# Moving three of twelve tiles from VectorE to ScalarE in a threshold search

## The chip, the cores and the metric

One core of one Trainium2 chip runs the kernel. The metric is the device time of one execution in microseconds (us), and lower is better. Three executions of the kernel before stand beside each other, with their median. A fourth was recorded by the profiler.

## What is computed

A block of a vision transformer: 64 images are cut into patches and embedded (37 tokens of 192 numbers each, 2368 tokens in all), attention is added, and then a mixture of 8 experts with two experts for each token. The part that the change touches decides which tokens an expert keeps:

```python
w = softmax(topv)                     # weights of the two chosen experts
priority = w[:, 0]
order = jnp.argsort(-priority)
...
pos = (jnp.cumsum(oh, axis=0) * oh).sum(-1) - 1
keep = pos < cap                      # cap = 740 tokens for each expert
```

An expert keeps its 740 tokens of highest priority. The kernel does not sort. For each expert it looks for the priority of the last token that is kept, as a number of six digits to the base 16, one digit at a level.

## The kernel before

The tokens lie in 22 tiles of 111 (`NG` tiles, `G` = 111; three images to a tile). Embedding and attention fill the first 360 us of the profile, the experts' two matrix products the time from about 418 us on. Between them lies the routing, a chain of short steps that hand over from engine to engine.

**The tables of the search.** For each of the 8 experts `mp` holds the priority of every token that chose it. `mpb` repeats each of these 16 times, so that 8 x 16 = 128 columns stand for (expert, trial digit). TensorE transposes `mpb` tile by tile (L935): a tile becomes 128 partitions by 111 tokens, and a semaphore, `s_mpt`, counts the tiles. Four tiles share a PSUM bank, in the order `TILE_BANKS`: tiles 0 to 3, 4 to 7 and 8 to 11 are in three neighbouring banks, tiles 12 to 21 in three others. VectorE owns the first twelve (`BY_DVE` = 12), ScalarE the last ten (`BY_ACT` = 10). ScalarE copies its ten out of PSUM into `mp_act` once, with three instructions (L1205), the last of which waits for tiles 20 and 21. Those two belong to the last attention step and come late (`EARLY` = 20).

**A level of the search** (`search`, six times, `LEVELS` = 6). In each partition there is a threshold `thr`. VectorE counts how many of its 1332 values exceed it (L1659, read straight from PSUM, the sum in `cnt`) and turns the count into a bar (L1662, `cnt_bar`). Beside it, ScalarE takes the sign of threshold minus value for its 1110 values and sums the signs (L1213, `sgn_sum`). VectorE waits for this sum and compares it with the bar (L1665, `enough`). TensorE adds the outcomes of a group up to the digit (L950, into PSUM), and VectorE makes the next threshold from it (L1657), which starts both engines on the next level. At the first level the threshold is ready long before, and ScalarE does one more thing behind its sum, the copy `ohe` (L1217). Between two digits TensorE runs five matmuls that nobody reads (`keep_warm`, L792).

**Behind the search** come the last threshold (L1672, L954), the comparison with it (L1677, L1678), the running counts on TensorE (L959, L963), the table of slots on VectorE and TensorE (L1681 to L1718, with L972), and then the gathers of the first expert's rows on GpSimd (L1936), which wait for the table `gid`. The order on each engine is that of the code. `junk_v` and `junk_a` take the elementwise results, which nobody reads. They, `mp_act` and a few other tables are cut one behind the other from one piece of SBUF that the trace calls `narrow`; other pieces are cut from one called `wide`.

Of the kernel before, what the change touches and what calls it, by code (L numbers as in the profile page):

```python
# [8 lines left out]
BF16 = mybir.dt.bfloat16  # L9
# [3 lines left out]
ALU = mybir.AluOpType  # L13
ACT = mybir.ActivationFunctionType
# [15 lines left out]
G = IPG * T  # L30
# [30 lines left out]
WAYS, LEVELS = 16, 6  # L61
LEAST = -0.25 - 2.0 ** -24
HALF_ULP = 2.0 ** -25
BY_DVE = 12
BY_ACT = NG - BY_DVE
EARLY = NG - 2
REPEATS_DVE = ((0, 6), (6, 12))
REPEATS_ACT = ((12, 16), (16, 20))
TILE_BANKS = (4, 5, 6, 2, 7, 0)
# [34 lines left out]
def build(nc, x, ln1_g, ln1_b, W_lin, b_lin, ln2_g, ln2_b, pos_embedding, cls_token,  # L104
# [7 lines left out]
    with ExitStack() as ctx:  # L112
# [5 lines left out]
        def early(name, shape, dt=F32):  # L118

            return phase.enter_context(nc.sbuf_tensor(name, shape, dt))  # L120

        def sem(name):
            return ctx.enter_context(nc.semaphore(name))

        PS = ctx.enter_context(nc.psum_tensor("PS", [128, 8, 512], F32))
# [45 lines left out]
        def carve(memory):  # L171

            at = [0]

            def piece(parts, n, dt=F32):
                words = n if dt is F32 else n // 2
                a, at[0] = at[0], at[0] + words
                assert at[0] <= memory.shape[1]
                v = memory[0:parts, a:a + words]
                return v if dt is F32 else v.bitcast(dt)  # L180
            return piece
# [3 lines left out]
        piece = carve(wide)  # L185
        wraw = piece(128, 3 * NQKV).rearrange("p (b n) -> p b n", b=3)
        piece = carve(wide)
# [10 lines left out]
        piece = carve(wide)  # L198
# [4 lines left out]
        piece = carve(wide)  # L203
# [60 lines left out]
        thr = early("thr", [128, LEVELS])  # L264
# [16 lines left out]
        piece = carve(narrow)  # L281
# [9 lines left out]
        piece = carve(narrow)  # L291
        onehot = piece(G, 2 * NG * 128, FP16).rearrange("p (n j) -> p n j", n=128)
        row_no = piece(G, 2 * NG * 128, FP16).rearrange("p (n j) -> p n j", n=128)
        ohe = piece(G, 2 * NG * E, FP16).rearrange("p (e k g) -> p e k g", e=E, k=2)
        junk_v = piece(128, BY_DVE * G, BF16)
        junk_a = piece(128, BY_ACT * G, BF16)
        mp_act = piece(128, BY_ACT * G)
        tid = piece(128, E * NT)
        tvoid = piece(128, E * NT)
# [106 lines left out]
        s_mpr = sem("member_prios_repeated")  # L406
        s_tail = sem("row_tails_ready")
        s_mpt = sem("member_prios_psum")
        s_sgn = sem("signs_summed")
        s_enough = sem("enough_ready")  # L410
        s_dig = sem("digit_psum")
# [33 lines left out]
        def bc(ap, shape):  # L445
            return ap.to_broadcast(shape)
# [633 lines left out]
        def _(act):  # L1080
# [5 lines left out]
            for u in range(UNITS):  # L1086
# [5 lines left out]
                if u in (UNITS - 2, UNITS - 1):  # L1092
                    n = u - (UNITS - 2)
# [22 lines left out]
            def outputs(s, g):  # L1116
                act.wait_ge(s_otp[g], s + 1)
                nc.scalar.copy(oTh[:, g, :].rearrange("p (a n) -> p a n", a=2),  # L1118
                               PS[:, (6, 4)[g]:(8, 6)[g], 0:3 * G]).then_inc(s_oth[g], 1)
# [6 lines left out]
            def probs(s, g):  # L1126
                act.wait_ge(s_sh[g], s + 1)

                nc.scalar.activation(
                    pb[:, g, :].rearrange("p (h i t) -> p h i t", h=H, i=IPG),  # L1130
                    bc(sc[:, g, :].rearrange("p (h a t) -> p h a t", h=H, a=1), [G, H, IPG, T]),
                    ACT.Exp).then_inc(s_p[g], 1)

            def gate_rows(s):
                act.wait_ge(s_xrp, s + 1)
                nc.scalar.copy(xnT[:, :, :].rearrange("p k n -> p (k n)"), PS[0:KD, 3, 0:2 * G2]).then_inc(s_xrT, 1)

            def logits(s):
                act.wait_ge(s_lp, s + 1)
                nc.scalar.copy(logit[:, bass.ds(2 * s, 2), :],  # L1140
                               PS[0:G, 3, 0:2 * E].rearrange("p (g e) -> p g e", g=2)).then_inc(s_l, 1)

            def gap_exp(b_, at):
                act.wait_ge(s_d, b_ + 1)
                nc.scalar.activation(ex[:, at], ex[:, at], ACT.Exp).then_inc(s_e, 1)

            def last_step():

                s = STEPS - 1
                logits(s - 1)  # L1150
                probs(s, 0)
                act.wait_ge(s_sh[1], s + 1)
                nc.scalar.activation(pb[0:T, 1, :].rearrange("p (h i t) -> p h i t", h=H, i=IPG)[:, :, 0, :],
                                     sc[0:T, 1, :].rearrange("p (h t) -> p h t", h=H), ACT.Exp).then_inc(s_p[1], 1)
                outputs(s, 0)
                act.wait_ge(s_otp[1], s + 1)
                nc.scalar.copy(oTh[:, 1, :].rearrange("p (a c n) -> p a c n", a=2, c=3)[:, :, :, 0:T],
                               PS[:, 4:6, 0:3 * G].rearrange("p a (c n) -> p a c n", c=3)[:, :, :, 0:T]
                               ).then_inc(s_oth[1], 1)
                gap_exp(0, slice(0, EARLY))  # L1160
                gate_rows(s)
                logits(s)
                act.wait_ge(s_mp, 1)
                for a, z in REPEATS_ACT:
                    nc.scalar.copy(mpb[:, a:z], bc(mp[:, a:z, :].rearrange("p g (e a) -> p g e a", a=1),
                                                   [G, z - a, E, WAYS])).then_inc(s_mpr, 1)
                gap_exp(1, slice(EARLY, NG))
# [6 lines left out]
            def step(s):  # L1174

                before_ = not is_step(s, 0)
                if before_:
                    probs(s - 1, 0)
                if before_ and not is_step(s, 1):
                    logits(s - 2)  # L1180
                queries(s, qr, rrb, s_qr)
                queries(s, qw, rwb, s_q)
                if before_:
                    probs(s - 1, 1)
                relative(s, 0)
                relative(s, 1)
                for g in range(2):
                    if before_:
                        outputs(s - 1, g)
                    values(s, g)  # L1190
                rows_transposed(s + 1)
                if before_:
                    gate_rows(s - 1)
# [5 lines left out]
            with act.Fori(2, STEPS) as s:  # L1199
                step(s)  # L1200
            last_step()
            for n, bank in ((4, TILE_BANKS[3]), (4, TILE_BANKS[4]), (2, TILE_BANKS[5])):
                t = 4 * TILE_BANKS.index(bank)
                act.wait_ge(s_mpt, t + n)
                last = nc.scalar.copy(mp_act[:, (t - BY_DVE) * G:(t - BY_DVE + n) * G], PS[:, bank, 0:n * G])  # L1205
            last.then_inc(s_mpr, 1)
            act.wait_ge(s_mpr, 3)
            for n in range(LEVELS):
                if n == 0:
                    act.wait_ge(s_ktab, 1)  # L1210
                else:
                    act.wait_ge(s_thr, n)
                nc.scalar.activation(junk_a[:, :], mp_act[:, :], ACT.Sign, bias=thr[:, n:n + 1], scale=-1.0,  # L1213
                                     accum_out=sgn_sum[:, n:n + 1]).then_inc(s_sgn, 1)
                if n == 0:
                    act.wait_ge(s_mp, 4)
                    nc.scalar.copy(ohe[:, :, :, :], oh[:, :, :, :].rearrange("p k g e -> p e k g")).then_inc(s_ohe, 1)  # L1217
# [82 lines left out]
        def _(dve):  # L1300
            v = nc.vector

            def ch(ins):

                dve.drain()
# [345 lines left out]
            def search(n):  # L1651

                if n == 0:
                    dve.wait_ge(s_mpt, BY_DVE)
                else:
                    dve.wait_ge(s_dig, n)
                    v.tensor_tensor(thr[:, n:n + 1], PS[:, 3, 0:1], try_at[:, n:n + 1], ALU.add).then_inc(s_thr, 1)  # L1657
                    dve.wait_ge(s_thr, n)
                ch(v.tensor_scalar(junk_v[:, :].rearrange("p (a n) -> p a n", a=BY_DVE // 4),  # L1659
                                   PS[:, TILE_BANKS[0]:TILE_BANKS[0] + BY_DVE // 4, 0:4 * G], thr[:, n:n + 1], None, ALU.is_gt, ALU.add,  # L1660
                                   accum_out=cnt[:, n:n + 1]))
                ch(v.tensor_scalar(cnt_bar[:, n:n + 1], cnt[:, n:n + 1], 2.0, float(BY_ACT * G - 2 * CAP),  # L1662
                                   ALU.mult, ALU.add))
                dve.wait_ge(s_sgn, n + 1)
                v.tensor_tensor(enough[:, n:n + 1], sgn_sum[:, n:n + 1], cnt_bar[:, n:n + 1], ALU.is_le  # L1665
                                ).then_inc(s_enough, 1)

            dve.wait_ge(s_ktab, 1)
            for n in range(LEVELS):
                search(n)  # L1670
# [367 lines left out]
```

## Time and profile before

| | us |
|---|---|
| three executions | 611.55, 611.6, 614.45 |
| their median | 611.6 |
| the profiled execution, whole | 611.77 |
| its span, first to last instruction | 610.0 |
| the search, first sum on ScalarE to last digit | 373.2 to 387.7 |
| TensorE busy over the span | 539.3 (88%) |
| VectorE busy | 441.9 (72%) |
| ScalarE busy | 261.1 (43%) |

The shares are averages over stages that have different limits. TensorE is busy for 88% of the span, but in the stretch of the search it runs mostly the idle matmuls. What a change to the search is worth has to be read from its own 14.5 us.

### The profile page before, as it was taken

To read this page: it belongs to the slowest core of one execution; us is meant where nothing else is said; L and a number is where in the kernel's file an instruction comes from. 1 tells how busy PE (TensorE), PEld (TensorE's weight loads), DVE (VectorE), ACT (ScalarE), POOL (GpSimd) and SP (SyncE) were. 2 spreads that over 40 slices of the span, in tenths; PEclk is the share of its full clock that TensorE was granted. 3 is DMA by queue.
4 is the path that set the end of the run, shared out by engine and by line. 5 is a ranking of instruction groups with operands and counts; after the bars stand their busy time and mean duration, and the time that the engine had idled before them with its cause. 6 is when DMAs were issued, how large, how long until landed. Compare 5 with 4: busy or idle time off the path is not lost.

```text
span 610.0 us, 12448 instructions
## 1 busy us (share of the span) xinstructions
PE 539.3 (88%) x4254; PEld 502.6 (82%) x4258; DVE 441.9 (72%) x1028; ACT 261.1 (43%) x428; POOL 220.8 (36%) x209
## 2 busy tenths in 40 slices
PE   2999687999999999999999786658999999999982
PEld 2999587999989989999899673446899999999982
DVE  7889956577687776776877757564877777877753
ACT  1222443244342543443435105404685595585560
POOL 0266510202102012021020115017688787777463
PEclk9999797899999999999999767869999999999997
DMA  8798535111201202102012018403466466357160
GB/s 204 171 219 255 139 72 135 24 36 17 51 19 32 51 3 48 36 15 51 23 29 51 2 33 214 129 5 107 125 159 160 103 139 151 94 128 153 19 170 31
DMA packets 62009, 54.97 MB, mean 90 GB/s; under 512 B 29204, under 2 KB 52564, under 8 KB 61182
## 3 DMA queue, kind: packets, MB, share of 16 engines
q1 hardware_dynamic: 52830, 46.04, 29.6%
q0 software_dynamic: 9152, 8.59, 8.2%
q8 instruction: 14, 0.23, 0.2%
q14 instruction: 13, 0.11, 0.1%
HBM read 39.32 MB, written 18.27 MB: 94 GB/s over the span
## 4 chain that ended last, share of the span: by engine, by line
PE 47%; DVE 14%; ACT 13%; issue 9%; SPq 5%; DMA 4%; POOL 3%; DVEq 2%; POOLq 1%; ACTq 0%
PE PS L1058 7%; PE PS L757 7%; PE PS L734 6%; PE PS L713 5%; ACT wide L1105 4%; PE PS L1056 4%; ACT hTh L1246 3%; PE PS L741 2%; PE PS L750 2%; PE PS L748 2%; PE PS L749 2%; DVE hTl L1753 2%; PE PS L721 2%; PE PS L728 2%; PE PS L1033 2%
## 5 line engine op out<-in xcount | busy, mean ns | idle before, releaser
L1828 POOL TENSOR_TENSOR rs<-ve,nhalf 111x1 f32<-111x1 f32 (+2 forms) x40 | 26.1, 653 | 272.4 <-DVE ve L1396 189.5
L1962 POOL DMA_INDIRECT running_sums<-ye,gid x42 | 74.5, 1774 | 30.8 <-DVE ye L1777 21.7
L1058 PE MATMUL PS<-w2hl,hTh 128*128 128x384 f32 (+1 forms) x288 | 82.7, 357 | 0.0
L1056 PE MATMUL PS<-w2hl,hTl 128*128 128x192 f32 (+1 forms) x288 | 73.4, 255 | 3.7 <-DVE hTl L1753 3.7
L1936 POOL DMA_INDIRECT xe<-routed_rows,gid x48 | 53.2, 1109 | 43.5 <-DVE gid L1718 28.9
L1056 PEld LDWEIGHTS PS<-w2hl,hTl 128*128 128x128 f32 (+1 forms) x288 | 53.7, 187 | 6.0 <-issue 5.2
L1033 PE MATMUL PS<-xeT,w1h 128*128 128x370 f32 x252 | 56.0, 330 | 0.0
L1058 PEld LDWEIGHTS PS<-w2hl,hTh 128*128 128x128 f32 (+1 forms) x288 | 53.0, 184 | 0.5
L713 PE MATMUL PS<-xT,wh 128*128 128x222 f32 x264 | 47.5, 290 | 6.5 <-DVE xT L1410 6.5
L1753 DVE TENSOR_TENSOR hTl<-hf,hTh 128x740 fp32r<-128x740 f32 x42 | 39.0, 928 | 19.4 <-ACT hTh L1246 18.3
L713 PEld LDWEIGHTS PS<-xT,wh 128*128 128x128 f32 x264 | 38.5, 201 | 8.7 <-issue 5.9
L1033 PEld LDWEIGHTS PS<-xeT,w1h 128*128 128x128 f32 x252 | 44.2, 188 | 0.0
L682 PE MATMUL PS<-narrow 128*128 128x192 f32 x216 | 41.0, 343 | 3.0 <-ACT narrow L1090 3.0
L1033 PE MATMUL PS<-xeT,w1l 128*128 128x370 f32 x168 | 42.0, 331 | 0.0
L734 PE MATMUL PS<-wide 111*111 111x96 f32 x336 | 39.8, 283 | 1.2 <-DVE wide L1549 1.2
L682 PEld LDWEIGHTS PS<-narrow 128*128 128x128 f32 x216 | 37.6, 203 | 3.3 <-ACT narrow L1090 3.3
L734 PEld LDWEIGHTS PS<-wide 111*111 111x111 f32 x336 | 37.9, 196 | 2.1 <-DVE wide L1549 1.3
L1243 ACT ACTIVATE hf<-PS,b1s 128x740 f32<-128x740 f32 x42 | 36.7, 875 | 6.1 <-PE PS L1033 4.0
L1428 DVE SCALAR_TENSOR_TENSOR wide<-PS,ind,wide 111x296 f32<-111x296 f32 x64 | 33.6, 525 | 4.2 <-issue 0.2
L713 PE MATMUL PS<-xT,wl 128*128 128x222 f32 x176 | 35.1, 282 | 0.0
L1118 ACT CAST oTh<-PS 128x666 fp32r<-128x666 f32 x21 | 15.1, 718 | 45.6 <-PE PS L741 45.6
L748 PE MATMUL PS<-woh,oTh 128*111 128x192 f32 x126 | 33.5, 266 | 0.9 <-DVE oTl L1458 0.9
(257 smaller groups left out, 1319.0 us busy)
## 6 DMA issues: line engine op xcount, KB each, us to landing
wide<-x SPq DMA_DIRECT2D x24, 288.0 KB, 9.2
w1r<-L_ffn_W SPq DMA_DIRECT2D x16, 384.0 KB
rel_scores<-wide SPq DMA_DIRECT2D x66, 73.0 KB
w2r<-L_ffn_W SPq DMA_DIRECT2D x8, 576.0 KB, 4.4
w1r<-L_ffn_W SPq DMA_DIRECT2D x16, 192.0 KB
wide<-rel_scores SPq DMA_DIRECT2D x22, 111.0 KB, 2.2
out<-running_sums SPq DMA_DIRECT2D x1, 1776.0 KB, 7.7
h_tokens<-narrow SPq DMA_DIRECT2D x24, 72.0 KB, 2.8
```

The source lines that it names most:

```text
L682: last = pe.matmul(PS[:, 4 + u % 4, 0:D], xTt[:, u % 2, c, :], W_cen[:, c, :], start=(c == 0), stop=(c == PC - 1))
L713: last = pe.matmul(PS[:, bank, (m % 2) * G2:(m % 2 + 1) * G2], lhsT, xT[:, b_, :], start=(nth == 0 and m % 2 == 0), stop=(nth == len(BLOCK ...
L734: last = pe.matmul(heads(4 - 2 * g, V)[:, j, :], pT[:, g, j * G:(j + 1) * G], v_sb[:, g, h * V:(h + 1) * V], start=(j % HB == 0), stop=Tru ...
L748: pe.matmul(PS[0:G, g, 0:D], oTh[:, g, at], woh[:, c, :], start=(c == 0), stop=False)
L757: last = pe.matmul(PS[0:G, 2 * g + n, 0:HB * V], xT[:, b_, g * G:(g + 1) * G], (wh, wl)[w][:, b_, at:at + HB * V], start=(nth == 0), stop= ...
L1033: last = pe.matmul(PS[:, hidden_bank(c) + n, 0:HALF], (w1h, w1l)[hl][:, b_, w], xeT[:, b_, n * HALF:(n + 1) * HALF], start=(nth == 0), sto ...
L1056: pe.matmul(PS[0:n, bank, 0:D], hTl[:, c, at], w2hl[:, c, 0, :], start=(c == 0), stop=False, skip_group_check=True)
L1058: last = pe.matmul(PS[0:n, bank, 0:2 * D], hTh[:, c, at], both(w2hl[:, c, :, :]), start=False, stop=(c == HC - 1), skip_group_check=True)
L1243: last = nc.scalar.activation(hf[:, c % 2, :].rearrange("p (a n) -> p a n", a=2), src, ACT.Gelu, bias=b1s[:, p, c:c + 1])
L1753: v.tensor_tensor(hTl[:, c, :], hf[:, c % 2, :], hTh[:, c, :].bitcast(F32), ALU.subtract).then_inc(s_hl, 1)
L1936: p_.indirect_dma_start(xe[0:r, p, n, :], None, xr_dram, bass.IndirectOffsetOnAxis(ap=gid[0:r, e, n:n + 1], axis=0), bounds_check=B * T - ...
L1962: p_.indirect_dma_start(sums, at, ye[0:r, e % 2, n, :], None, bounds_check=B * T + NT * 128 - 1, oob_is_err=True, compute_op=ALU.add).then ...
```

## The change

`BY_DVE` goes from 12 to 9 and so `BY_ACT` from 10 to 13. VectorE now counts the first three tiles of each of its three banks, 9 x 111 = 999 values. The fourth tile of each bank (tiles 3, 7 and 11) goes to ScalarE, which copies the three with one instruction ahead of its other copies. VectorE's first count waits for that copy (`s_fourth`) in place of the twelfth transpose. ScalarE's sum covers 1443 values. The two junk tiles get one spare element, since their lengths are odd now. The constant in `cnt_bar` follows from `BY_ACT`.

```diff
-BY_DVE = 12
+BY_DVE = 9
 BY_ACT = NG - BY_DVE
...
+        s_fourth = sem("fourth_tiles_copied")
...
             last_step()
+            act.wait_ge(s_mpt, 12)
+            nc.scalar.copy(mp_act[:, 0:3 * G].rearrange("p (a n) -> p a n", a=3),
+                           PS[:, TILE_BANKS[0]:TILE_BANKS[0] + 3, 3 * G:4 * G]).then_inc(s_fourth, 1)
             for n, bank in ((4, TILE_BANKS[3]), (4, TILE_BANKS[4]), (2, TILE_BANKS[5])):
...
-                nc.scalar.activation(junk_a[:, :], mp_act[:, :], ACT.Sign, bias=thr[:, n:n + 1], scale=-1.0,
+                nc.scalar.activation(junk_a[:, 0:BY_ACT * G], mp_act[:, :], ACT.Sign, bias=thr[:, n:n + 1], scale=-1.0,
                                      accum_out=sgn_sum[:, n:n + 1]).then_inc(s_sgn, 1)
...
                 if n == 0:
-                    dve.wait_ge(s_mpt, BY_DVE)
+                    dve.wait_ge(s_fourth, 1)
...
-                ch(v.tensor_scalar(junk_v[:, :].rearrange("p (a n) -> p a n", a=BY_DVE // 4),
-                                   PS[:, TILE_BANKS[0]:TILE_BANKS[0] + BY_DVE // 4, 0:4 * G], thr[:, n:n + 1], None, ALU.is_gt, ALU.add,
+                ch(v.tensor_scalar(junk_v[:, 0:BY_DVE * G].rearrange("p (a n) -> p a n", a=3),
+                                   PS[:, TILE_BANKS[0]:TILE_BANKS[0] + 3, 0:3 * G], thr[:, n:n + 1], None, ALU.is_gt, ALU.add,
                                    accum_out=cnt[:, n:n + 1]))
```

On ScalarE, from the exponent of the last two tiles to the first cast of the experts' weights, the kernel before has these instructions in a row (`narrow` written from `PS` is `mp_act`, `narrow` written from `narrow` the junk, `sgn_sum` the sums):

```order
L1145 ACTIVATE ex<-ex 111x2
L1205 COPY narrow<-PS 128x444 x2
L1205 COPY narrow<-PS 128x222
L1213 ACTIVATE narrow,sgn_sum<-narrow,thr 128x1110
L1217 CAST narrow<-oh 111x352
L1213 ACTIVATE narrow,sgn_sum<-narrow,thr 128x1110 x5
L1223 CAST w1h<-w1r 128x2304
```

At the same place the changed kernel has these, with line numbers moved by the added lines:

```order
L1146 ACTIVATE ex<-ex 111x2
L1204 COPY narrow<-PS 128x333
L1209 COPY narrow<-PS 128x444 x2
L1209 COPY narrow<-PS 128x222
L1217 ACTIVATE narrow,sgn_sum<-narrow,thr 128x1443
L1221 CAST narrow<-oh 111x352
L1217 ACTIVATE narrow,sgn_sum<-narrow,thr 128x1443 x5
L1227 CAST w1h<-w1r 128x2304
```

One copy of 333 values stands ahead of the three others, and the six sums are longer by 333 values; nothing else changes its place. VectorE and TensorE keep every instruction where it was.

## Rows read from the trace of the kernel before

**Rows 1.** The page: its span, and the chain that ended last, by engine.

```profile
span 610.0 us, 12448 instructions
PE 47%; DVE 14%; ACT 13%; issue 9%; SPq 5%; DMA 4%; POOL 3%; DVEq 2%; POOLq 1%; ACTq 0%
```

**Rows 2.** The chain in order of time, through the search: start us, us, what.

```profile
372.35 0.42 PE PS L935 x2
372.80 0.35 ACT narrow L1205
373.17 1.32 ACT narrow L1213 x2
374.52 0.17 DVE enough L1665
...
374.95 0.17 DVE thr L1657
375.15 1.60 DVE narrow L1659
...
377.06 0.17 DVE enough L1665
...
377.51 0.17 DVE thr L1657
...
385.15 0.17 DVE thr L1657
```

**Rows 3.** VectorE's timeline: start us, us, instruction, shapes [idle before, releaser].

```profile
372.21 1.60 DVE L1659 TENSOR_SCALAR_CACHE_REDUCE narrow<-PS,thr 128x1332 bf16<-128x1332 f32 x1
...
374.52 0.16 DVE L1665 TENSOR_TENSOR enough<-sgn_sum,cnt_bar 128x1 bf16<-128x1 f32 x1 [0.47 <-ACT narrow L1213]
```

**Rows 4.** ScalarE's timeline, around the first level and at the sixth.

```profile
369.65 0.52 ACT L1205 COPY narrow<-PS 128x444 f32<-128x444 f32 x1
370.38 0.53 ACT L1205 COPY narrow<-PS 128x444 f32<-128x444 f32 x1 [0.21 <-PE PS L935]
372.80 0.34 ACT L1205 COPY narrow<-PS 128x222 f32<-128x222 f32 x1 [1.89 <-PE PS L935]
373.17 1.22 ACT L1213 ACTIVATE narrow<-narrow,thr 128x1110 bf16<-128x1110 f32 x1
374.30 0.19 ACT L1213 ACTIVATION_READ_ACCUMULATOR narrow<-narrow,thr 128x1 f32 x1
374.39 0.81 ACT L1217 CAST narrow<-oh 111x352 f16<-111x352 f32 x1
375.15 1.22 ACT L1213 ACTIVATE narrow<-narrow,thr 128x1110 bf16<-128x1110 f32 x1
...
385.35 1.22 ACT L1213 ACTIVATE narrow<-narrow,thr 128x1110 bf16<-128x1110 f32 x1 [1.24 <-DVE thr L1657]
386.47 0.19 ACT L1213 ACTIVATION_READ_ACCUMULATOR narrow<-narrow,thr 128x1 f32 x1
```

**Rows 5.** Groups by shape, VectorE, PSUM operand: line, shapes, count, busy us, mean ns.

```profile
L1442 DVE TENSOR_TENSOR wide<-PS,block 111x888 f32<-111x888 f32 x20 | 21.6, 1079 | 5.3 <-PE PS L728 5.3
L1409 DVE TENSOR_TENSOR xT<-PS,xT 128x222 fp32r<-128x222 f32 x12 | 4.6, 382 | 5.1 <-ACT xT L1098 5.0
```

**Rows 6.** Groups by shape, ScalarE.

```profile
L1205 ACT COPY narrow<-PS 128x444 f32<-128x444 f32 x2 | 1.0, 524 | 0.2 <-PE PS L935 0.2
L1205 ACT COPY narrow<-PS 128x222 f32<-128x222 f32 x1 | 0.3, 343 | 1.9 <-PE PS L935 1.9
L1243 ACT ACTIVATE hf<-PS,b1s 128x740 f32<-128x740 f32 x42 | 36.7, 875 | 6.1 <-PE PS L1033 4.0 <-DVE hTl L1753 2.0
```

**Rows 7.** Stretches behind the search: busy us (count) of PE, PEld, DVE, ACT, POOL, granted clock, DMA share, GB/s.

```profile
388.00:393.00 5.00, 4.32 (x26) 3.58 (x27) 0.81 (x4) 4.65 (x4) 0.00 (x0) 0.66 0.13 37
407.00:412.00 5.00, 3.49 (x9) 1.34 (x10) 3.37 (x9) 0.00 (x0) 2.69 (x2) 0.50 0.07 19
420.00:430.00 10.00, 8.77 (x53) 8.14 (x52) 8.29 (x20) 9.26 (x23) 7.57 (x7) 1.00 0.60 166
```

**Rows 8.** The chain and GpSimd's timeline behind the search.

```profile
389.50 3.25 PE PS L963 x22
409.00 1.81 POOL L1936 DMA_INDIRECT xe<-routed_rows,gid  x1 [28.93 <-DVE gid L1718]
```

More of the change, by code:

```diff
@@ L294, in build @@
         ohe = piece(G, 2 * NG * E, FP16).rearrange("p (e k g) -> p e k g", e=E, k=2)
-        junk_v = piece(128, BY_DVE * G, BF16)
-        junk_a = piece(128, BY_ACT * G, BF16)
+        junk_v = piece(128, BY_DVE * G + 1, BF16)
+        junk_a = piece(128, BY_ACT * G + 1, BF16)
         mp_act = piece(128, BY_ACT * G)
```

## The prediction

> **What bounds the kernel now.** I read the page first, for its span and its chain by engine [rows 1]: TensorE's 47% is work of other stages, so it says nothing on the search. Then I followed the chain in order of time through the search [rows 2]. The reader is to see that it changes hands. At the first level it comes from TensorE's last transposes through ScalarE's last copy and its sum. From the second level on it stays on VectorE: threshold, count, comparison, digit, next threshold. So the first level waits for ScalarE and the five others for VectorE. The two timelines confirm it. At the first level VectorE's count starts at 372.21, ScalarE's sum only at 373.17, and the comparison sits idle for 0.47 us until the sum is there [rows 3, 4]. At the sixth level ScalarE has its sum at 386.47 + 0.19 = 386.66, after it had itself waited 1.24 us for the threshold [rows 4].
>
> Last I looked at what follows. GpSimd waited 28.93 us for the slot table before its first gather [rows 8], so the routing as a whole sets when the experts' stage begins, and what the search saves should reach the end of the kernel.
>
> **The length of a level before.** Thresholds begin at 374.95, 377.51 and 385.15, the last being four levels after the first: (385.15 - 374.95) / 4 = 2.55 us a level [rows 2]. Of it the two legs that run beside each other take the part from the threshold to the comparison. VectorE's leg: 374.95 to 377.06, 2.11 us [rows 2]. ScalarE's leg: its sum starts 385.35 - 385.15 = 0.20 us after the threshold [rows 2, 4], the sum and its reading take 386.66 - 385.35 = 1.31 us [rows 4], and at the first level, where VectorE really waits for it, the comparison follows 0.03 us after the reading (374.30 + 0.19 = 374.49 against 374.52) [rows 3, 4]. Together 0.20 + 1.31 + 0.03 = 1.54 us. ScalarE has 2.11 - 1.54 = 0.57 us to spare.
>
> **VectorE's leg, shorter by 333 values.** The trace has no count of 999 values. Two groups of another operation from PSUM give the price of one more value: (1079 - 382) / (888 - 222) = 1.047 ns [rows 5]. The count itself gives the upper bound, 1.60 us / 1332 = 1.20 ns, if nothing in it were fixed [rows 3]. I take the slope of the two groups, since it leaves the fixed part out: 333 x 1.047 = 0.35 us (at most 0.40). The leg becomes 2.11 - 0.35 = 1.76 us.
>
> **ScalarE's leg, longer by 333 values.** From 222 to 444 values a copy grows by (524 - 343) / 222 = 0.815 ns a value [rows 6], and from the 740 values of a Gelu to the 1110 of the sum it is (1222 - 875) / 370 = 0.94 ns, across two kinds of instruction [rows 4, 6]. The sum in proportion, 1222 / 1110 = 1.10 ns, is the upper bound. I take 0.83, near the first, because it comes from one instruction at two sizes: d = 333 x 0.83 = 0.28 us, between 0.27 and 0.37. The leg becomes 1.54 + 0.28 = 1.82 us, and is now the later of the two by 0.06.
>
> Here a rule speaks against the change. The Trainium skill, page "ScalarE: Activation LUTs", section "Rules for kernel authors", sends simple elementwise work to VectorE, which it calls up to about 3 times faster per element in bf16. By it a moved value would save only a third of 0.83 ns on VectorE, 333 x 0.28 = 0.09 us a level, and the sum below would be 5 x 0.09 - 0.28 = 0.17 us. The trace disagrees for this source: 1.047 ns on VectorE against 0.815 on ScalarE. The skill's page "VectorE: DVE Perf Modes", section "Why PSUM operands drop a tier", gives the reason, fp32 from PSUM at one value a cycle.
>
> **The sum.** Levels 2 to 6 each gain 2.11 - 1.82 = 0.29 us: 5 x 0.29 = 1.45. Level 1 was ScalarE's already and loses d = 0.28. Net gain 1.17 us. With d = 0.27 it is 5 x 0.30 - 0.27 = 1.23, and with d = 0.37 it is 5 x 0.20 - 0.37 = 0.63.
>
> **What costs nothing, and what covers it.** The added copy of 333 values lies between 343 and 524 ns, some 0.43 us [rows 6]. It runs at about 369.65 and pushes the two copies behind it; the second of them ended at 370.38 + 0.53 = 370.91 and ScalarE then sat idle for 1.89 us until the last transposes [rows 4]. The idle time takes it, with over 1.4 us left. Without that cover the first level would be later by 0.43.
>
> VectorE's new wait for the copy is over at about 370.1, and its first count started at 372.21 for other reasons [rows 3]; queued behind it are only this level's own comparison and all that follows, which wait for ScalarE anyway. Since ScalarE ends the level at about 374.8, the count may start over 1 us late at no cost.
>
> The copy `ohe` behind the first sum ends at 374.39 + 0.81 = 375.20, and the second sum starts at 375.15 [rows 4], as early as the threshold allows (374.95 + 0.20). Both move by d, so at the second level it costs at most the 0.05 by which it overlaps. Behind the search ScalarE's next work is the cast of the weights, which is not needed before the rows are gathered. The odd lengths and the moved tables in SBUF I price at nothing: no work is added by them.
>
> **Rivals.** First, the clock behind the search. In 388 to 393 us the mean granted clock is 0.66, that is, some 3.4 of the 5 us at the lower of the two levels (1.2 GHz) and the rest at 2.4 GHz [rows 7]; the running counts lie there (3.25 us) [rows 8]. If they came 1.2 us sooner and found the higher level throughout, they would take up to 1.7 us less: 611.6 - 1.2 - 1.7 = 608.7. For it: the search leaves TensorE less idle time per level. Against it: the idle matmuls per level are the same five, and the higher level was already granted through the end of the search only to fall here.
>
> Second, the same mechanism with the other sign, slower than before. From 407 to 412 the clock is at the lower level, from 420 to 430 at the higher [rows 7]. If the level rises later relative to the program, the experts' first products run slow. A stretch of 3.4 us at the lower level, as the one above, does 1.7 us' worth of work, so it costs 1.7: 611.6 - 1.2 + 1.7 = 612.1. Two such stretches give 613.8, and the kernel is slower by over 0.5% only from three of them on. It decides against the change from 2 x 1.2 = 2.4 us of product work at the lower level. Against it: the rise came before the first product here, and TensorE's work ahead of it keeps its order.
>
> Third, the change doesn't shorten VectorE's leg, because a count over three pieces is bound by something other than its values. Then the levels stay at 2.11 us and level 1 loses 0.28: 611.9. Against it: the pieces were three before too.
>
> **How the numbers follow.** The profiled execution took 611.77 us, of which 610.0 were span [rows 1]; 1.17 less is 610.6. It stood 0.17 above the median of the three runs, 611.6, against which I forecast: 611.6 - 1.2 = 610.4. Its own bounds by d are 610.4 and 611.0. Chances: this sum 0.72, the clock's gain 0.10 (down to 608.7), the clock's loss 0.10 (612.1 and above), no shorter leg 0.08 (611.9, or 611.4 by the page's rule). The three runs before lie between 611.55 and 614.45, so a median can sit some tenths from its case. The range reaches down to 609.0 and up to 612.3, which leaves out the far ends of the clock's two cases.
>
> About 0.5% (3.1 us) is what a measurement of this kernel can tell from no change; 1.2 us is 0.2%. So no change by that bound has 0.94. Faster by more needs the whole of the clock's gain and some more, 0.03; slower by more needs three slow stretches, 0.03.
>
> **What would show it.** In the profile after: VectorE's count near 1.25 us and ScalarE's sum near 1.50; thresholds 2.26 us apart; from level 2 on, the comparison idle for about 0.06 us on ScalarE's sum instead of none; at level 1 idle for about 1.1 us (0.47 + 0.35 + 0.28); the digit of the last level about 1.2 us sooner; the first gather sooner by as much. I would be wrong if the count kept its 1.60 us, if the sum took more than 1.22 + 0.48 = 1.70 us (5 x (0.57 - d) = d gives d = 0.475, where the gain is gone), or if the first gather is sooner but the experts' stage ends no sooner.

## The result, and the profile after

The changed kernel takes 609.69 us (median of 20 executions, 608.11 to 612.84) against 611.58 us for the kernel before (20 executions on the same chips). The ratio is 0.9962, with a 95% interval of 0.9949 to 0.9976: faster by 1.5 to 3.1 us, most likely 2.3 (the medians alone differ by 1.9). A second measurement of the same two kernels gave 0.9980 (0.9965 to 0.9995): faster by 0.3 to 2.1 us, most likely 1.2. What both intervals hold is 1.5 to 2.1 us, some 0.3%. That is no change by the bound of 0.5% and lies in the forecast range. The first measurement is above the 1.2 us of the forecast, the second is centred on it, so the totals leave open whether there is more. The ratios of this document are formed from undisturbed executions; one execution of e12, 871 us at a mean granted clock of 0.56, is left out.

First the profile's page of the changed kernel, span and chain by engine, which answers to [rows 1]:

```profile
span 607.8 us, 12453 instructions
PE 48%; ACT 14%; DVE 13%; issue 9%; SPq 5%; DMA 4%; POOL 3%; DVEq 2%; POOLq 1%; ACTq 0%
```

ScalarE's share has risen by one point and VectorE's fallen by one. Where that comes from, the chain in order of time shows (start us, us, what), to be held against [rows 2]:

```profile
371.77 0.42 PE PS L936 x2
...
372.22 0.35 ACT narrow L1209
...
372.60 1.60 ACT narrow L1217 x2
...
374.22 0.17 DVE enough L1669
...
374.63 2.16 PE PS L793 x5
376.78 0.12 PE PS L951
...
376.92 0.17 DVE thr L1661
...
377.11 1.60 ACT narrow L1217 x2
378.74 0.17 DVE enough L1669
...
379.17 0.17 DVE thr L1661
...
379.36 1.60 ACT narrow L1217 x2
380.96 0.02 issue
380.99 0.17 DVE enough L1669
```

VectorE's count has gone from the chain. ScalarE's sum ends last at the first level, where it did before, and from the third level on too. At the second the profile leads the chain through the five idle matmuls: the granted clock is at its lower level there, they take 2.16 us, and the digit comes right behind them. This cost next to nothing (thresholds at 374.66 and 376.92, 2.26 us), but the kernel before had 0.52 us between them and the digit; a level much shorter than this would wait for them. Thresholds follow each other after 2.25 us (376.92 to 379.17) in place of 2.55. VectorE's timeline (start us, us, instruction, shapes, idle before it) shows by how little it comes second:

```profile
371.64 1.25 DVE L1663 TENSOR_SCALAR_CACHE_REDUCE narrow<-PS,thr 128x999 bf16<-128x999 f32 x1
...
374.22 0.16 DVE L1669 TENSOR_TENSOR enough<-sgn_sum,cnt_bar 128x1 bf16<-128x1 f32 x1 [1.09 <-ACT narrow L1217]
...
377.12 1.26 DVE L1663 TENSOR_SCALAR_CACHE_REDUCE narrow<-PS,thr 128x999 bf16<-128x999 f32 x1
378.30 0.08 DVE L1663 DVE_READ_ACCUMULATOR narrow<-PS,thr 128x1 f32 x1
378.46 0.15 DVE L1666 TENSOR_SCALAR cnt_bar<-cnt 128x1 f32<-128x1 f32 x1
378.74 0.16 DVE L1669 TENSOR_TENSOR enough<-sgn_sum,cnt_bar 128x1 bf16<-128x1 f32 x1
```

From the end of the bar, 378.46 + 0.15 = 378.61, to the comparison there are now 0.13 us; in the run below in which VectorE has the last word it is 0.07 (376.79 + 0.15 to 377.01). So VectorE is done some 0.06 us before ScalarE. At the first level it waits for 1.09 us. ScalarE's timeline, to be held against [rows 4]:

```profile
369.08 0.42 ACT L1204 COPY narrow<-PS 128x333 f32<-128x333 f32 x1
369.40 1.05 ACT L1209 COPY narrow<-PS 128x444 f32<-128x444 f32 x2
372.22 0.34 ACT L1209 COPY narrow<-PS 128x222 f32<-128x222 f32 x1 [1.77 <-PE PS L936]
372.60 1.50 ACT L1217 ACTIVATE narrow<-narrow,thr 128x1443 bf16<-128x1443 f32 x1
374.00 0.19 ACT L1217 ACTIVATION_READ_ACCUMULATOR narrow<-narrow,thr 128x1 f32 x1
```

The added copy takes 0.42 us, and ScalarE still waits 1.77 us for the last transposes behind it. The sum takes 1.50 us in place of 1.22.

**Where the time went.** The two profiled spans differ by 610.0 - 607.8 = 2.2 us. I divide them at four instructions: the first sum, VectorE's use of the last digit, the slot table `gid`, and the first product of the experts.

| us | before | after | difference |
|---|---|---|---|
| start to first sum | 373.17 | 372.60 | -0.57 |
| search: first sum to last digit's use | 14.53 | 13.32 | -1.21 |
| last digit's use to slot table | 20.14 | 19.64 | -0.50 |
| slot table to first product | 10.50 | 10.81 | +0.31 |
| first product to end | 191.66 | 191.43 | -0.23 |

The search gained what the forecast said. Half a microsecond more came behind it, where nothing was edited. Granted clocks there (busy us and count of PE, PEld, DVE, ACT, POOL, then clock, DMA share, GB/s), first in the changed kernel, then in the kernel before, to be held against [rows 7]:

```profile
385.00:387.00 2.00, 0.54 (x2) 0.27 (x2) 1.07 (x7) 0.45 (x2) 0.00 (x0) 1.00 0.99 304
387.00:388.00 1.00, 0.82 (x6) 0.77 (x7) 0.12 (x1) 0.87 (x1) 0.00 (x0) 1.00 0.85 237
388.00:391.00 3.00, 3.00 (x21) 2.55 (x20) 0.44 (x3) 2.98 (x3) 0.00 (x0) 0.52 0.05 15
```

```profile
388.50:388.80 0.30, 0.00 (x0) 0.00 (x0) 0.30 (x2) 0.30 (x1) 0.00 (x0) 0.95 0.43 127
388.80:389.00 0.20, 0.04 (x1) 0.04 (x1) 0.10 (x1) 0.20 (x1) 0.00 (x0) 0.50 0.29 79
```

The running counts (L960, L964) begin at 387.18 and the clock falls to the lower level just behind 388: they have some 0.9 us of the higher level. Before, they began at 388.96, when it had just fallen. They take 3.31 us in place of 3.81. Measured from the first sum, the fall comes at nearly the same place, 15.6 us after it before and 15.5 now, and the counts begin 15.8 and 14.6 us after it. Whether this half microsecond belongs to the change, and whether the 0.57 us ahead of the search do, was the question for the runs.

### The profile page after: what moved, and what is told of

It reads as the page before. It is cut to its first block, busy times and chain, and to the rows that moved or that the text cites. A ratio compares the mean times of both kernels' runs of the same rounds, so it can differ in the third digit from the quotient of the medians.

```text
span 607.8 us, 12453 instructions
## 1 busy us (share of the span) xinstructions
PE 540.1 (89%) x4258; PEld 502.9 (83%) x4258; DVE 439.7 (72%) x1028; ACT 263.1 (43%) x429; POOL 220.4 (36%) x209
## 4 chain that ended last, share of the span: by engine, by line
PE 48%; ACT 14%; DVE 13%; issue 9%; SPq 5%; DMA 4%; POOL 3%; DVEq 2%; POOLq 1%; ACTq 0%
PE PS L1059 7%; PE PS L758 7%; PE PS L735 6%; PE PS L714 5%; ACT wide L1106 4%; PE PS L1057 4%; ACT hTh L1250 3%; PE PS L742 2%; PE PS L749 2%; PE PS L751 2%; PE PS L750 2%; DVE hTl L1757 2%; PE PS L722 2%; PE PS L729 2%; DVEq L1309 2%
```

## The experiments

Theory A: the change acts by the two legs of a level alone, and beyond the search it only moves the running counts relative to the clock's fall. Theory B: the time ahead of the search belongs to it too. In the table all runs are divided at the same instructions as above; "counts" is the part of the third column from the first running count (L959 in the kernel before) to VectorE's first look at it (L1681), and the sum is that of search, third and fifth column. Starts are from the timelines of one profiled execution each. The ratio is to the kernel before on the same chip.

| run | search | to slot table | counts | to first product | sum | ratio (95%) |
|---|---|---|---|---|---|---|
| before | 14.53 | 20.14 | 3.81 | 10.50 | 45.17 | |
| e1 before, again | 14.53 | 20.65 | 4.15 | 10.42 | 45.60 | 1.0007 (0.9993 to 1.0021) |
| after | 13.32 | 19.64 | 3.31 | 10.81 | 43.77 | 0.9962 (0.9949 to 0.9976) |
| e2 after, again | 13.33 | 19.61 | 3.30 | 10.50 | 43.44 | 0.9980 (0.9965 to 0.9995) |
| e3 VectorE alone | 12.79 | 19.30 | 2.99 | 10.57 | 42.66 | 0.9960 (0.9943 to 0.9977) |
| e4 ScalarE alone | 14.82 | 20.65 | 4.15 | 10.56 | 46.03 | 1.0020 (1.0002 to 1.0038) |
| e5 copy late | 13.39 | 20.22 | 3.90 | 10.55 | 44.16 | 0.9977 (0.9958 to 0.9996) |
| e6 six and sixteen | 14.99 | 20.67 | 4.15 | 10.52 | 46.18 | 1.0007 (0.9989 to 1.0025) |
| e7 warm tail | 13.32 | 18.58 | 2.26 | 9.61 | 41.51 | 0.9925 (0.9903 to 0.9947) |
| e8 first level | 13.05 | 19.62 | 3.30 | 10.42 | 43.09 | 0.9953 (0.9934 to 0.9972) |
| e9 before, warm tail | 14.52 | 18.57 | 2.25 | 9.55 | 42.64 | 0.9937 (0.9915 to 0.9959) |
| e10 e8 with e7 | 13.03 | 18.57 | 2.25 | 9.58 | 41.18 | 0.9927 (0.9899 to 0.9955) |
| e11 four behind | 13.32 | 19.68 | 3.35 | 9.61 | 42.61 | 0.9956 (0.9939 to 0.9974) |
| e12 four moved | 13.33 | 18.57 | 2.26 | 10.40 | 42.30 | 0.9943 (0.9924 to 0.9962) |

### e1 and e2: both kernels again

> The kernel before, unchanged, for a second profile. Theory A (only the search and the place of the clock's fall behind it belong to the change): a ratio of 1.000 to itself, thresholds 2.55 us apart, and a first threshold level that starts anywhere within some tenths of 373.2 us, since the 0.57 us by which the changed kernel was ahead at that point is a difference between executions. Theory B (the 0.57 us ahead of the search belong to the change too, by way of the tables moved in SBUF): ScalarE's first sum starts at 373.2 again, within 0.1 us.

> The changed kernel, unchanged, for a second profile. Theory A: thresholds 2.25 us apart, the search (ScalarE's first sum to the last digit's use on VectorE) 13.3 us against 14.5; the start of the first sum differs from 372.6 by some tenths, and the running counts take 3.3 us only if the clock falls as late relative to them as in the first profile (else up to 3.8, or down to 2.2). Ratio near 0.997. Theory B: the first sum starts at 372.6 again and the running counts take 3.3 us again; ratio 0.996.

The search repeats to 0.01 us in both kernels. The first sum starts at 373.26 in e1 and 373.24 in e2, so theory B falls: the changed kernel is not ahead at that point. Over the fourteen profiles this start lies anywhere from 371.0 to 374.1, and most of the spread is there early: ScalarE's cast of `woh` starts between 87.0 and 89.4. What follows from it: 0.57 of the 2.2 us between the first two profiles were no part of the change.

In e1 the clock fell earlier and was lower for longer. Granted clocks of e1, same columns:

```profile
385.00:387.00 2.00, 1.98 (x6) 0.60 (x6) 1.73 (x3) 1.31 (x2) 0.00 (x0) 0.54 0.96 257
387.00:389.00 2.00, 1.01 (x3) 0.36 (x2) 0.92 (x7) 0.88 (x1) 0.00 (x0) 0.50 0.81 232
389.00:392.00 3.00, 2.77 (x12) 2.44 (x13) 0.17 (x1) 2.98 (x3) 0.00 (x0) 0.50 0.03 8
392.00:394.50 2.50, 2.50 (x17) 1.67 (x16) 0.97 (x4) 0.79 (x2) 0.00 (x0) 0.50 0.00 0
```

It fell as the last level of the search began, and the whole of the running counts, 389.23 to 393.38, ran at the lower level: 4.15 us. So the stretch behind the search costs 20.14 or 20.65 us before and 19.6 after, a further gain of 0.5 to 1.0 us in these four profiles.

### e3 and e4: one engine's part alone

```diff
 e3, on the kernel before
-                ch(v.tensor_scalar(junk_v[:, :].rearrange("p (a n) -> p a n", a=BY_DVE // 4),
-                                   PS[:, TILE_BANKS[0]:TILE_BANKS[0] + BY_DVE // 4, 0:4 * G], ...
+                ch(v.tensor_scalar(junk_v[:, 0:9 * G].rearrange("p (a n) -> p a n", a=3),
+                                   PS[:, TILE_BANKS[0]:TILE_BANKS[0] + 3, 0:3 * G], ...
 e4, on the changed kernel
-        junk_v = piece(128, BY_DVE * G + 1, BF16)
+        junk_v = piece(128, 12 * G, BF16)
...
-                ch(v.tensor_scalar(junk_v[:, 0:BY_DVE * G].rearrange("p (a n) -> p a n", a=3),
-                                   PS[:, TILE_BANKS[0]:TILE_BANKS[0] + 3, 0:3 * G], ...
+                ch(v.tensor_scalar(junk_v[:, :].rearrange("p (a n) -> p a n", a=3),
+                                   PS[:, TILE_BANKS[0]:TILE_BANKS[0] + 3, 0:4 * G], ...
```

> The kernel before, but VectorE counts nine tiles and ScalarE its ten: tiles 3, 7 and 11 are left out of the search, so that other tokens are kept. Theory A: the five levels that VectorE bounds get shorter by 0.35 us each, to 2.20 us, the first level (ScalarE's) keeps its 1.35 us from sum to comparison; 1.75 us less in the search, 609.8. Rival (the count over three pieces is bound by something else): levels stay at 2.55.

> The changed kernel, but VectorE counts all twelve tiles as before: tiles 3, 7 and 11 are counted twice, so that other tokens are kept. ScalarE's longer sums stand alone. Theory A: the first level is longer by 0.28 us, the five others stay at 2.55, since VectorE's leg of 2.11 still ends behind ScalarE's 1.82; search 14.8 us, total 0.3 above the kernel before (611.9). Rival (the two engines disturb each other, and the gain came from elsewhere): the levels change by more than 0.05 us.

VectorE's timeline of e3, its second level:

```profile
375.25 0.16 DVE L1657 TENSOR_TENSOR thr<-PS,try_at 128x1 f32<-128x1 f32 x1 [0.27 <-PE PS L950]
375.44 1.26 DVE L1659 TENSOR_SCALAR_CACHE_REDUCE narrow<-PS,thr 128x999 bf16<-128x999 f32 x1
376.62 0.08 DVE L1659 DVE_READ_ACCUMULATOR narrow<-PS,thr 128x1 f32 x1
376.79 0.15 DVE L1662 TENSOR_SCALAR cnt_bar<-cnt 128x1 f32<-128x1 f32 x1
377.01 0.16 DVE L1665 TENSOR_TENSOR enough<-sgn_sum,cnt_bar 128x1 bf16<-128x1 f32 x1
```

VectorE's leg is 377.01 - 375.25 = 1.76 us, the forecast number, and levels take 2.20 us; the search is 1.74 us shorter against 1.75 expected. In e4 the first level is longer by 0.27 and the others stay at 2.55; the search is 0.29 us longer against 0.28 expected. Both rivals fall: the count is bound by its values, (1.60 - 1.26) / 333 = 1.02 ns each, and the levels show no sign that the engines disturb each other. The total of e4 seems to rise by more than the search (1.0020, some 1.2 us, though its interval begins at 0.1); its profile shows the counts at the lower clock, as in e1.

### e5: the copy without its cover

```diff
-            act.wait_ge(s_mpt, 12)
-            nc.scalar.copy(mp_act[:, 0:3 * G].rearrange("p (a n) -> p a n", a=3),
-                           PS[:, TILE_BANKS[0]:TILE_BANKS[0] + 3, 3 * G:4 * G]).then_inc(s_fourth, 1)
             for n, bank in ((4, TILE_BANKS[3]), (4, TILE_BANKS[4]), (2, TILE_BANKS[5])):
...
             last.then_inc(s_mpr, 1)
+            last = nc.scalar.copy(mp_act[:, 0:3 * G].rearrange("p (a n) -> p a n", a=3),
+                                  PS[:, TILE_BANKS[0]:TILE_BANKS[0] + 3, 3 * G:4 * G])
+            last.then_inc(s_fourth, 1)
+            act.wait_ge(s_fourth, 1)
```

> The changed kernel with the copy of the fourth tiles moved behind the three other copies, where nothing hides it. Theory A: ScalarE's first sum starts 0.33 to 0.43 us later relative to the last transposes, and nothing else moves; the total is 0.3 to 0.4 us above the changed kernel. VectorE's first count waits for the copy too, which costs nothing, since ScalarE ends this level by over 1 us. Rival (the copy was not hidden): no difference.

ScalarE's timeline of e5:

```profile
371.74 0.35 ACT L1206 COPY narrow<-PS 128x222 f32<-128x222 f32 x1 [1.50 <-PE PS L936]
371.98 0.44 ACT L1208 COPY narrow<-PS 128x333 f32<-128x333 f32 x1
372.45 1.50 ACT L1218 ACTIVATE narrow<-narrow,thr 128x1443 bf16<-128x1443 f32 x1
```

The last transposes start at 371.29, the first sum 1.16 us later; in the changed kernel it is 372.60 - 371.77 = 0.83. So the bare copy costs 0.33 us, as expected. VectorE's late count cost 0.06 us on top (1.68 us from the sum to the comparison in place of 1.62), where I had expected that it costs nothing. The ratio can't tell a third of a microsecond: the clock's stretch differs by more between executions (counts of 3.90 here).

### e6: as far again

```diff
-BY_DVE = 9
+BY_DVE = 6
...
-            nc.scalar.copy(mp_act[:, 0:3 * G].rearrange("p (a n) -> p a n", a=3),
-                           PS[:, TILE_BANKS[0]:TILE_BANKS[0] + 3, 3 * G:4 * G]).then_inc(s_fourth, 1)
+            nc.scalar.copy(mp_act[:, 0:6 * G].rearrange("p (a n) -> p a n", a=3),
+                           PS[:, TILE_BANKS[0]:TILE_BANKS[0] + 3, 2 * G:4 * G]).then_inc(s_fourth, 1)
...
-                                   PS[:, TILE_BANKS[0]:TILE_BANKS[0] + 3, 0:3 * G], ...
+                                   PS[:, TILE_BANKS[0]:TILE_BANKS[0] + 3, 0:2 * G], ...
```

> The split moved as far again: VectorE counts six tiles, ScalarE sums sixteen and copies six. Theory A: each sum is longer by another 0.28 us (1.78 us), ScalarE bounds all six levels, 2.25 + 0.28 = 2.53 us a level, VectorE's count takes 0.91 us and its comparison waits 0.7 us; search 13.3 + 6 x 0.28 = 15.0 us, which is 1.7 above the changed kernel and 0.5 above the one before: about 612. Rival (fewer values on VectorE are what helps, whatever ScalarE does): below the changed kernel.

VectorE's timeline of e6, the comparison at the second level:

```profile
377.39 0.16 DVE L1669 TENSOR_TENSOR enough<-sgn_sum,cnt_bar 128x1 bf16<-128x1 f32 x1 [0.75 <-ACT narrow L1217]
```

Count 0.91, sum 1.78, levels 2.53, idle 0.75 us: all as expected, and the search of 14.99 us is 0.46 longer than before. Fewer values on VectorE don't help by themselves. ScalarE's price is (1.78 - 1.50) / 333 = 0.84 ns a value at both steps, so nine and thirteen tiles lie near the balance.

### e7 and e9: TensorE kept busy behind the search

```diff
-  keep_warm(5 if n < LEVELS - 1 else 0, 1)
+  keep_warm(5 if n < LEVELS - 1 else 1, 1)
...
   pe.transpose(PS[0:G, 3, 128:256], bc(last_in[:, :], [128, G]), ident[:, :]).then_inc(s_dig, 1)
+  keep_warm(3, 1)
```

e7 has this edit on the changed kernel, e9 on the kernel before.

> The changed kernel with four more idle matmuls on TensorE: one behind the last digit, three behind the transpose of the last threshold, in gaps in which it had nothing to do. Theory A with the clock (the running counts are short or long by the level that they find, and idle time ahead of them brings the fall): the clock stays at its higher level through the running counts, which take 2.2 us in place of 3.3; total 1.1 us less, 608.6. Rival (the fall doesn't hang on these gaps): running counts 3.3 to 3.8 us, and the total as it was or up to 0.2 more, if an idle matmul delays what follows.

> The kernel before with the four idle matmuls of the run with the warm tail, so that both splits can be compared with the running counts at the higher clock. Theory A (beyond the search the change only moves the running counts relative to the clock's fall): counts of 2.3 us here too, search still 14.53 us, total about 1.5 us below the kernel before (610.2), so that the change is worth 1.2 us, the search alone, between the two kernels with the warm tail. Rival (the shorter levels of the changed kernel are what holds the clock up, and the four matmuls work only with them): counts of 3.3 to 4.2 us, total as before.

The granted clock of e7 in the stretch of the counts (385.61 to 387.87), and the counts in the chains of e7 and of e9:

```profile
385.00:389.00 4.00, 3.97 (x33) 2.71 (x32) 1.54 (x6) 3.26 (x3) 0.00 (x0) 1.00 0.38 110
```

```profile
385.61 0.36 PE PS L961
385.97 1.88 PE PS L965 x22
```

```profile
389.05 0.36 PE PS L960
389.40 1.88 PE PS L964 x22
```

With the gaps filled the clock stays at the higher level, and the counts take 2.26 us, in the kernel before as well (2.25). So the rival that the four matmuls work only with the shorter levels falls. The Trainium skill, page "TensorE: Matmul & The Clock Gate", section "What's actually happening", describes the lower clock as the default state that activity releases; these rows agree as far as they go, with a granted clock of 1.00 and counts of 2.25 us where the gaps are filled, 0.50 and 4.15 us in e1 where they are idle. And with the clock equal, the change is worth the search alone: from e9 to e7 the sum falls by 42.64 - 41.51 = 1.13 us, with 1.20 in the search. This is read from the stages of one profile each; the two totals (0.9937 and 0.9925, on different chips) can't tell it.

Whether the shorter levels by themselves help to keep the clock up is not shown. In e1, e4 and e6 it fell during the search, some 12 us after the first sum; these are three of the five profiles with levels of 2.5 us or more. In none of the nine profiles with levels of 2.20 to 2.26 us did it fall so early.

Both totals fell by more than expected (607.57 us against 608.6 in e7, 608.60 against 610.2 in e9). A part is that the time from slot table to first product came down by 0.9 us as well, which I had not expected (e11 and e12).

### e8 and e10: the first level by its own split

```diff
-        junk_v = piece(128, BY_DVE * G + 1, BF16)
+        junk_v = piece(128, 12 * G, BF16)
...
-                nc.scalar.activation(junk_a[:, 0:BY_ACT * G], mp_act[:, :], ACT.Sign, ...
+                skip = 0 if n else 3 * G
+                nc.scalar.activation(junk_a[:, skip:BY_ACT * G], mp_act[:, skip:], ACT.Sign, ...
...
-                ch(v.tensor_scalar(junk_v[:, 0:BY_DVE * G].rearrange("p (a n) -> p a n", a=3),
-                                   PS[:, TILE_BANKS[0]:TILE_BANKS[0] + 3, 0:3 * G], ...
+                w = 3 * G if n else 4 * G
+                ch(v.tensor_scalar(junk_v[:, 0:3 * w].rearrange("p (a n) -> p a n", a=3),
+                                   PS[:, TILE_BANKS[0]:TILE_BANKS[0] + 3, 0:w], ...
...
-                ch(v.tensor_scalar(cnt_bar[:, n:n + 1], cnt[:, n:n + 1], 2.0, float(BY_ACT * G - 2 * CAP),
+                ch(v.tensor_scalar(cnt_bar[:, n:n + 1], cnt[:, n:n + 1], 2.0, float((BY_ACT if n else BY_ACT - 3) * G - 2 * CAP),
```

e8 has this edit on the changed kernel, e10 this one and that of e7.

> The changed kernel, but the first level is split as before: VectorE counts twelve tiles (it had 1.09 us to spare there), ScalarE sums ten. Theory A: the first level gets its 0.28 us back and the others keep theirs; search 13.05 us; total 0.3 us below the changed kernel. Rival (the first level's loss is hidden by something else, the copy behind the first sum): no difference in the search.

> The changed kernel with both additions, the first level split twelve to ten and the warm tail. Theory A: search 13.05 us, counts 2.3 us; total 0.3 us below the run with the warm tail alone and some 3 us below the kernel before, about 608.4 to 608.8. Rival (the two don't add): no lower than either.

The search falls by the 0.27 us that the first level had lost, to 13.05 and 13.03 us. In the total this is not to be seen: e10 (608.78 us, 6 executions) and e7 (607.57 us, 6) have intervals that overlap nearly whole. Both are faster than the kernel before; against the changed kernel only e7's interval lies clear of both measurements. By its stages e10 is the shortest of all, 41.18 us against 45.17 and 45.60.

### e11 and e12: the clock, or the number of instructions

In all three runs with the warm tail the first product came 9.6 us after the slot table, in the others at least 10.4. The queue of instruction loads (q8) differs there too: one packet lies 5.5 to 6.5 us behind the slot table in all runs without the warm tail up to then, and 1.0 to 1.5 us behind it in those with it.

```diff
 e11, on the changed kernel
-            keep_warm(20, 1)
+            keep_warm(24, 1)
 e12, on e7
-            keep_warm(20, 1)
+            keep_warm(16, 1)
```

> The changed kernel with the four extra idle matmuls behind the running counts (24 there in place of 20), where they can't help the clock ahead of the counts. In the runs with the warm tail the first product also came 0.9 us sooner after the slot table, and the packet of the instruction queue that lay 4 to 8 us behind the slot table came with it. Theory I (four more instructions of TensorE bring its next load of instructions forward, out of the wait for the gathers): slot table to first product 9.6 us, counts still 3.3 us; total about 0.9 below the changed kernel. Theory C (the clock does it): 10.5 us, no gain.

> The changed kernel with the warm tail, but with 16 idle matmuls behind the running counts in place of 20, so that TensorE has as many instructions up to the gathers as the changed kernel. Theory I (instruction load): counts 2.25 us by the clock, but slot table to first product 10.5 us as in the changed kernel; total about 1.0 below the changed kernel. Theory C: 9.6 us, total 1.9 below.

The two came apart. In e11 the counts stay at 3.35 us and the first product comes at 9.61; in e12 the counts take 2.26 us and the first product comes at 10.40. So it is the number of TensorE's instructions ahead of the gathers, not its clock. This rests on one profile each, but all fourteen sort the same way: 9.55 to 9.61 us with four more instructions, 10.40 to 10.81 us without. The totals of e11 and e12 can't tell them apart, since their intervals overlap. The chain's wait for the gathered rows, in the changed kernel, in e11 and in e12 (start us, us, what):

```profile
410.15 3.86 DMA xe<-routed_rows,gid
```

```profile
409.72 2.65 DMA xe<-routed_rows,gid
```

```profile
410.14 3.45 DMA xe<-routed_rows,gid
```

And the DMA queues (packets, MB, share of the 16 engines' time): e11 from 1 us ahead of the slot table to 2 us behind it, then e11 and e12 from 4 to 6 us behind it:

```profile
q8 instruction: 1, 0.02, 1.9%
```

```profile
q0 software_dynamic: 73, 0.12, 23.2%
```

```profile
q0 software_dynamic: 77, 0.13, 23.0%
q8 instruction: 1, 0.02, 3.5%
```

In e11 the instruction packet is past (at 406.1 to 406.6 us) before any gathered row moves (behind 408.6), and from 4 to 6 us there are gathers alone. In e12 it falls among them. Four instructions more bring it forward into the time before the rows move, and 0.8 to 1.2 us go. What TensorE waits for is the third tile, and the time from issue to landing tells that these rows do come late: 3.5 to 3.9 us for the third gather in the ten runs whose packet falls among the gathers, 2.6 to 2.7 in the four others, while the second gather takes 2.6 to 2.7 on both sides. So TensorE does not merely wait for its own instructions here. That it is the packet that holds up the rows is the likely reading; no run moved the packet by other means.

## Why the prediction was right

**The legs were right, each to 0.02 us.** VectorE's leg was forecast at 1.76 us and measured 1.76 (e3). Count 1.25 (1.26), sum 1.50 (1.50), threshold to threshold 2.26 (2.25), idle at the first level 1.1 (1.09), VectorE ahead by 0.06 (0.06). The slope from two other operations, 1.047 ns, held for the count (1.02), and the 0.83 ns for the sum (0.84).

**The sum was right for the search**, 1.17 against 1.21 us. So was the loss at the first level, 0.28 against 0.27 (e4, e8).

**The cover was right.** The copy cost nothing where it stands and 0.33 us where it is bare (e5), against the 0.43 that I gave as its price. Instructions that follow each other without a wait overlap (in e5 the copy starts at 371.98, the one ahead of it ends at 371.74 + 0.35 = 372.09), so the whole duration was too much. Against the 0.33, the late count of e5 added 0.06 us that I had put at nothing.

**The term that was mis-sized is what follows the search.** In the sum I carried it at nothing and gave the clock's gain a chance of 0.10 as a case of its own, of up to 1.7 us. A gain of this kind was there in both profiles of the changed kernel, with 0.5 to 1.0 us. Against the first profile of the kernel before, the reason is that a chain that comes 1.2 us sooner has more of its counts ahead of a fall that stayed where it was; against e1 the fall itself had also come earlier, and why is open. I had argued against the clock's gain that the clock falls here anyway; it does, but a part of the work now lies before it. The first rival was therefore no alternative to the sum but an addition to it. 1.2 and 0.5 to 1.0 us, less up to 0.3 for the gathers, are 1.4 to 2.2 us, and the two measurements have 1.5 to 2.1 in common, though the second alone would fit the bare 1.2 as well. That the total stayed in the range is owed in part to its lower end, 609.0, which I had drawn for a case that I held unlikely. With the clock held up on both sides (e9 against e7), the stages leave about the forecast sum, 1.13 us.

**"The first gather sooner by as much" was too simple a sign.** It starts 409.00 - 406.71 = 2.29 us sooner, of which 0.57 came before the search by chance.

**The rivals.** The slower clock under the experts' products did not occur: the higher level was back at 409 and 410 us in the two profiles of the changed kernel, and the first product came at 416 and 417. The unshortened leg fell with e3. The rule of the Trainium skill's page "ScalarE: Activation LUTs", section "Rules for kernel authors", that would send elementwise work to VectorE, and that the page states for bf16, does not carry over to these fp32 values: 1.02 ns a value from PSUM on VectorE (e3), 0.84 on ScalarE (e6). For ScalarE the Trainium skill's page "ScalarE: Activation LUTs", section "What ACT_TABLE_LOAD costs", gives 0.833 ns a value, and the trace agrees with its 0.84.

## What to carry to other kernels

Where two engines work beside each other, write down both legs from the common start to the common end, and move work until they are equal; a row for the slope of each engine is enough to place the split, and the step that already waits for the receiving engine loses and wants a split of its own. A copy that is made once was free where it stood ahead of a wait, and cost most of its duration behind it (0.33 of 0.44 us). Idle matmuls that fill a gap have to fit into it at the lower clock too: five of them took 2.16 us here, nearly a whole level of 2.25. A short serial chain behind idle time of TensorE runs at whichever clock it finds, so look at the granted clock of the stretch behind the edit before calling it unchanged: here four idle matmuls in gaps were worth more than the split, by the stages of the profiles.

## What the runs showed of the hardware that was not expected

Four extra matmuls anywhere between the last digit and the gathers shortened a wait that is put down to the gathers by 0.8 to 1.2 us (e7, e9, e10, e11 against e12 and the others), together with the place of one packet of the instruction queue. The rows themselves landed later, 3.5 to 3.9 us after their issue in place of 2.6 to 2.7. So the length of a DMA went here with the number of instructions that an engine had in its program ahead of it.

The running counts, 23 small matmuls, took 2.25 us with the clock at 2.4 GHz throughout and 4.15 us at 1.2 GHz, and anything between where the clock changed in their midst. The same program, the kernel before, met different places of the fall in two executions (3.81 and 4.15 us).
